# The last stage of a two-layer decoder: order of TensorE's products, statistics one step ahead, scores by chunks, and an output bias added by TensorE

## The reference

```
z      = layernorm(x)                      # only ahead of the first of the two
logits = compete_w . rms(z) + b            # 16 slots, per token
w      = softmax over tokens, of the 4 largest of each slot, else 0
ws     = rms(workspace + write(w . z))     # 16 x 512, the slots' content
att    = softmax(q(z) . k(ws)), 8 heads    # 128 tokens x 16 slots each
y      = z + out_proj(att . v(ws)) + out_b # out_b: the output bias
z'     = rms(y) * norm_post                # after the second: x + z' is stored
```

## Time and profile before

| | us |
|---|---|
| median of three timed runs | 4096.97 (4094.72 to 4097.59) |
| profiled execution | 4095.58 |
| its span | 4093.8 |
| last stage, TensorE busy in steps 1 to 15 | 803.30 of 936.90 |

### The profile page before, as it was taken

One profiled execution on the slowest core, in us unless ns is written; L12 is line 12 of the kernel. 1 busy time (PEld: TensorE's weight loads), 2 busy tenths in 40 slices (PEclk: granted clock), 3 DMA queues, 4 the chain that ended last, 5 costly groups with the idle time before them and its releaser, 6 DMA issues. The chain is left out here.

```text
span 4093.8 us, 86187 instructions
## 1 busy us (share of the span) xinstructions
PE 3644.9 (89%) x24323; PEld 1810.7 (44%) x24323; DVE 2875.2 (70%) x4470; ACT 2573.2 (63%) x6419; POOL 1785.7 (44%) x2216
## 2 busy tenths in 40 slices
PE   5999999999999994899999799999958878888886
PEld 1222222222222221778778444444436555465563
DVE  5888888888888883677777577777744454444545
ACT  2777777777777774677777577777734434344352
POOL 6444444444444430666665122222222543545535
PEclk9999999999999997899999999999979999999998
DMA  7777777777777762333332233333340120211102
GB/s 115 121 125 120 124 122 123 124 120 125 122 120 125 121 94 85 101 113 112 114 114 87 78 94 94 93 95 95 94 141 1 47 78 2 88 38 62 63 1 78
DMA packets 342548, 385.78 MB, mean 94 GB/s; under 512 B 58432, under 2 KB 223040, under 8 KB 342336
## 3 DMA queue, kind: packets, MB, share of 16 engines
q1 hardware_dynamic: 315712, 348.69, 39.4%
q10 hardware_dynamic: 26624, 34.63, 3.3%
HBM read 196.52 MB, written 84.93 MB: 69 GB/s over the span
## 5 line engine op out<-in xcount | busy, mean ns | idle before, releaser
L302 DVE TENSOR_REDUCE a_neg_max<-a_max_ps 128x2 f32<-128x1024 f32 x1024 | 1201.0, 1219 | 194.6 <-PE a_max_ps L354 169.8
L380 ACT ACTIVATE a_P<-a_ring_ps 128x512 f32<-128x512 f32 x2048 | 1084.6, 604 | 382.0 <-PE a_ring_ps L336 378.2
L354 PE MATMUL a_max_ps<-a_K,a_Q 96*128 96x512 bf16 x2048 | 621.1, 385 | 44.0 <-DMA a_K<-a_k_split 39.8
L336 PE MATMUL a_ring_ps<-a_Q,a_K 98*128 98x512 bf16 x2048 | 617.5, 382 | 5.7 <-DMA a_Q<-a_max_rows 3.5
L365 PE MATMUL a_pv_ps<-a_P,a_V 128*32 128x512 f32 x4096 | 544.9, 604 | 1.8 <-ACT a_out_sb L385 1.8
L336 PEld LDWEIGHTS a_ring_ps<-a_Q,a_K 98*128 98x128 bf16 x2048 | 158.9, 96 | 659.5 <-ACT a_P L380 585.5
L1163 ACT ACTIVATE c_P<-c_s_ps,c_bias 128x128 f32<-128x128 f32 x1024 | 361.5, 367 | 138.9 <-DVE c_bias L1035 130.2
L1092 PE MATMUL c_s_ps<-c_KD,c_qT 128*128 128x512 f32 x512 | 276.7, 622 | 33.5 <-ACT c_qT L1154 28.3
L1834 ACT ACTIVATE d_junk<-d_y 128x512 bf16<-128x512 f32 x128 | 80.6, 630 | 341.7 <-DVE d_y L1524 341.7
L256 POOL TENSOR_SCALAR a_var_eps<-a_mean_var 128x1 f32<-128x1 f32 x64 | 12.2, 190 | 648.1 <-DVE a_mean_var L318 647.9
L1031 DVE TENSOR_REDUCE c_neg_max<-c_s_ps 128x4 f32<-128x512 f32 x256 | 175.4, 685 | 163.7 <-PE c_s_ps L1093 163.7
(11 more groups left out here) (240 smaller groups left out, 7187.5 us busy)
## 6 DMA issues: line engine op xcount, KB each, us to landing
a_Q<-a_q_split SPq DMA_DIRECT2D x384, 128.0 KB
a_K<-a_k_split SPq DMA_DIRECT2D x384, 128.0 KB
heads_out<-a_out_sb ACTq DMA_DIRECT2D x128, 256.0 KB, 2.3
a_x_in<-in_x_dram SPq DMA_DIRECT2D x64, 256.0 KB, 3.6
a_c_in<-in_ctx_dram SPq DMA_DIRECT2D x64, 256.0 KB
a_cT_in<-in_ctxT_dram SPq DMA_DIRECT2D x64, 256.0 KB
b_x_in<-in_x_dram SPq DMA_DIRECT2D x64, 256.0 KB, 2.7
b_o_in<-heads_out SPq DMA_DIRECT2D x64, 256.0 KB
```

The costliest lines, as they stand in the source:

```text
L302: dve.tensor_reduce(neg_max[:, p, 2 * u:2 * u + 2], max_ps[u % 2][:, :, :], AX.X, ALU.max, negate=True).then_inc(max_taken, 1)
L336: pe.matmul(ring(s, use_of(k))[:, :], K[i][:, h, n:n + 128], Q[i][:, h, :], start=True, stop=True).then_inc(scores_filled, 1)
L354: last = pe.matmul(max_ps[u % 2][:, j, :], Q[i][0:KROW, h, m:m + 128], K[i][0:KROW, h, :], start=True, stop=True)
L380: act.activation(P[p][k // NT][:, k % NT, :], ring(s, use_of(k))[:, :], ACT.Exp, scale=SCALE).then_inc(exp_done, 1)
```

## The change

The bias add on GpSimd and its semaphore go; out_b is split at the start into three bf16 rows (at partitions 0, 32 and 64 of a 96-row tile that is otherwise 0), and each `mix` begins with a product of a 96 x 128 tile of ones with them, into the same bank, on which the f32 product accumulates. The layernorm statistics of a first f are made at the end of the step before; z is written in two halves, the first ahead of softmax(0). The scores go chunk by chunk (c outside, batch inside), and wait for six copies of A, for the last chunk for eight; the banks of the even and odd chunks change places (even now SC, odd F). On TensorE value_out(3) and mix(2) stand ahead of the wait for w_top, value_out(4) ahead of that for WT, mix(6) ahead of that for ws, mix(7) ahead of that for wsT; on VectorE final(6) and residual(7) stand ahead of kd, final(7) ahead of vd; ScalarE's copies and squares follow. Left out below: declarations, two memsets, and changed counts of `preset` and `const_ready`.

```diff
-body(Unit(0, k, 0), Unit(0, k, 1))
+body(Unit(0, k, 0), Unit(0, k, 1), Unit(0, k, -1))
...
-        + [(a_done, 2 * CK, i) for i in (0, 1, 4, 5)])
+        + [(a_done, 2 * CK, i) for i in (2, 3, 6, 7)])
...
-            add_bias(u, 0)
-            add_bias(u, 1)
         for b in range(NB):
-            if u.exists() and b >= 2:
-                add_bias(u, b)
             if u.exists() and b >= 1:
                 finish(u, b - 1)
...
-    def add_bias(u, b):
-
-        i, n = u.pair(), u.n()
-        if b == 0:
-            at_least(held, gT_done, n * 2 + 2)
-            at_least(held, xT_done, n * NB + NB)
-            if u.second():
-                held.wait_ge(x_sq_done, u.eight() * NB + NB)
-            held.wait_ge(g_done, n * 2 + 2)
-        pool.tensor_tensor(X[i][:, b, :], X[i][:, b, :], out_b_row[:, :], ALU.add).then_inc(x_biased, 1)
-        held.wait_ge(x_biased, n * NB + (b + 1))
...
+    dve.tensor_copy(out_b_part[:, :], out_b_row[0:96, :]).then_inc(const_ready, 1)
+    dve.wait_ge(const_ready, 4)
+    dve.tensor_copy(out_b_parts[0:1, :], out_b_part[0:1, :]).then_inc(const_ready, 1)
+    dve.tensor_tensor(out_b_row[0:96, :], out_b_row[0:96, :], out_b_part[:, :], ALU.subtract).then_inc(const_ready, 1)
+    dve.wait_ge(const_ready, 6)
+    dve.tensor_copy(out_b_part[:, :], out_b_row[0:96, :]).then_inc(const_ready, 1)
+    dve.wait_ge(const_ready, 7)
+    dve.tensor_copy(out_b_parts[32:33, :], out_b_part[32:33, :]).then_inc(const_ready, 1)
+    dve.tensor_tensor(out_b_row[0:96, :], out_b_row[0:96, :], out_b_part[:, :], ALU.subtract).then_inc(const_ready, 1)
+    dve.wait_ge(const_ready, 9)
+    dve.tensor_copy(out_b_parts[64:65, :], out_b_row[64:65, :]).then_inc(const_ready, 1)
...
+    def moments_of(f):
+
+        e = f.eight()
+        dve.wait_ge(x_loaded[f.pair()], f.turn() * 128 + 128)
+        at_least(dve, z_done, e * NB)
+        at_least(dve, x_ms_done, f.n())
+        for b in range(NB):
+            dve.bn_stats(stats[:, b, :], X[f.pair()][:, b, :]).then_inc(stats_done, 1)
+        for b in range(NB):
+            held.wait_ge(stats_done, e * NB + (b + 1))
+            dve.bn_aggr(moments[:, b, :], stats[:, b, :]).then_inc(moments_done, 1)
+    moments_of(Unit(0, 0, 0))
...
-            dve.wait_ge(x_biased, m + 1)
             dve.wait_ge(xb_filled, m + 1)
...
+        def normalise(batches):
+
+            dve.wait_ge(rstd_done, f.eight() + 1)
+            for b in batches:
+                dve.tensor_scalar(X[f.pair()][:, b, :], X[f.pair()][:, b, :], moments[:, b, 0:1], rstd[:, b:b + 1],
+                                  ALU.subtract, ALU.mult).then_inc(z_done, 1)
+
         first = f.exists() and not f.second()
         if first:
-
-            e = f.eight()
-            dve.wait_ge(x_loaded[f.pair()], f.turn() * 128 + 128)
-            at_least(dve, z_done, e * NB)
-            for b in range(NB):
-                dve.bn_stats(stats[:, b, :], X[f.pair()][:, b, :]).then_inc(stats_done, 1)
-            for b in range(NB):
-                held.wait_ge(stats_done, e * NB + (b + 1))
-                dve.bn_aggr(moments[:, b, :], stats[:, b, :]).then_inc(moments_done, 1)
+            normalise(range(0, NB // 2))
         if u.exists():
             softmax(0)
         if first:
-
-            dve.wait_ge(rstd_done, e + 1)
-            for b in range(NB):
-                dve.tensor_scalar(X[f.pair()][:, b, :], X[f.pair()][:, b, :], moments[:, b, 0:1], rstd[:, b:b + 1],
-                                  ALU.subtract, ALU.mult).then_inc(z_done, 1)
+            normalise(range(NB // 2, NB))
         if u.exists():
             softmax(1)
...
             residual(6)
+            final(6)
+            residual(7)
...
-            final(6)
-            residual(7)
+            final(7)
...
-        if u.exists():
-            final(7)
+        if after.exists() and not after.second():
+            moments_of(after)
...
-            pe.matmul(xb_ps[b % 2][:, :], attT[b // 4][:, b % 4, :], VO[b % 2][:, :], start=True, stop=True).then_inc(xb_filled, 1)
+            pe.matmul(xb_ps[b % 2][:, :], ones_rows[:, :], out_b_parts[:, :], start=True, stop=False)
+            pe.matmul(xb_ps[b % 2][:, :], attT[b // 4][:, b % 4, :], VO[b % 2][:, :], start=False, stop=True).then_inc(xb_filled, 1)
...
-                pe.wait_ge(a_done, n * 2 * CK + 2 * CK)
-                for b in range(half * 4, half * 4 + 4):
-                    for c in range(CK):
+                for c in range(CK):
+                    pe.wait_ge(a_done, n * 2 * CK + (8 if c == 3 else 6))
+                    for b in range(half * 4, half * 4 + 4):
                         last = pe.matmul(SC[half][:, b % 4 * 128:(b % 4 + 1) * 128], XT[i][:, c, b, :],
-                                         A[:, c, b].rearrange("p c s -> p (c s)"), start=(c == 0), stop=(c == CK - 1))
+                                         A[:, c, b].rearrange("p c s -> p (c s)"), start=(c == 0 and b % 4 == 0), stop=(c == CK - 1 and b % 4 == 3))
...
             mix(1)
+            value_out(3)
+            mix(2)
         if f.exists():
             ft = bank(pe, f, U_WT)
             pe.wait_ge(w_top_done, n * 2 + 2)
             pe.transpose(ft[:, 0:128], w_top[:, :], identf[:, :]).then_inc(wT_filled, 1)
         if u.exists():
-            value_out(3)
-            mix(2)
...
+            value_out(4)
...
-            value_out(4)
             mix(3)
...
             value_out(7)
+            mix(6)
...
-            mix(6)
+            mix(7)
         if f.exists():
             pe.wait_ge(wsT_done, n + 1)
             project(U_K, wk_sb)
-        if u.exists():
-            mix(7)
-        if f.exists():
             project(U_V, wv_sb)
...
-                pair = SC if c % 2 else [bank(pe, f, U_A + c + h) for h in range(2)]
-                if c == 3:
-                    pe.wait_ge(a_done, n * 2 * CK + 4)
+                pair = [bank(pe, f, U_A + c - 1 + h) for h in range(2)] if c % 2 else SC
+                if c == 2:
+                    pe.wait_ge(a_done, n * 2 * CK + 2)
...
+            values(3)
             squares(1)
-            values(3)
-            squares(2)
...
-            values(4)
+            squares(2)
+            values(5)
             squares(3)
-            values(5)
             squares(4)
...
             values(6)
+            values(7)
             squares(5)
-            values(7)
...
-                                   (SC[h] if c % 2 else F[(U_A + c + h) % 3])[:, :].rearrange("p (c b s) -> p c b s", c=CK, b=NB), ACT.Copy).then_inc(a_done, 1)
+                                   (F[(U_A + c - 1 + h) % 3] if c % 2 else SC[h])[:, :].rearrange("p (c b s) -> p c b s", c=CK, b=NB), ACT.Copy).then_inc(a_done, 1)
```

More of the change, by code:

```diff
@@ L1249, in workspace_ffn @@
         ws_first = sb("ws_first", [128, C])
+        out_b_parts, ones_rows = sb("out_b_parts", [96, C], BF16), sb("ones_rows", [96, 128], BF16)
+        out_b_part = sb("out_b_part", [96, C], BF16)
         neg_half = sb("neg_half", [128, NB])
@@ L1353, in _, with step @@
                 sp.sem_inc(out_stored[i], 16)
-            def step(f, u):
+            def step(f, u, after):
                 if u.exists() and u.second():
@@ L1378, in _ @@
             n = 0
-            for dst, value in ((neg_half[:, :], -0.5), (cw[:, :, :], 0.0), (lg[:, 128:136], -FAR), (chosen[:, :], -FAR), (WT[:, :, :], 0.0),
+            for dst, value in ((neg_half[:, :], -0.5), (cw[:, :, :], 0.0), (lg[:, 128:136], -FAR), (chosen[:, :], -FAR), (WT[:, :, :], 0.0), (out_b_parts[:, :], 0.0), (ones_rows[:, :], 1.0),
                                (vd[0][:, :, :, :, :], 0.0), (vd[1][:, :, :, :, :], 0.0)):
@@ L1482, in _ @@
             dve.wait_ge(small_in, 16 * (7 + 2 * NB))
-            dve.wait_ge(preset, 7)
+            dve.wait_ge(preset, 9)
             dve.tensor_tensor(cw[:, :, 0:S], cw_in[:, :, :], pre_col[:, :].unsqueeze(2).to_broadcast([128, CK, S]), ALU.mult).then_inc(const_ready, 1)
@@ L1657, in _, with step @@
         def _(pe):
-            pe.wait_ge(const_ready, 3)
-            def step(f, u):
+            pe.wait_ge(const_ready, 10)
+            def step(f, u, after):
                 def value_out(b):
@@ L1879, in step @@
                 if u.exists():
+                    values(3)
                     squares(1)
-                    values(3)
-                    squares(2)
+                    values(4)
                 if f.exists():
```

8 lines of the change are left out of this document (4 added, 4 removed).

## The result

Median 4041.59 us (four runs, 4037.83 to 4044.45) against 4097.28 for the kernel before on the same chip: a ratio of 0.9864 (95% interval 0.9848 to 0.9879), 55.7 us less, where 70 were forecast. The profiled execution took 4037.83 around a span of 4036.0, 57.8 shorter than the earlier trace rows.

The account below looks back on a forecast made before the run. Bound: a ring through VectorE, ScalarE and GpSimd, 3.6 us a turn, with TensorE's holes worth filling only down to it. 58.4 + 14.7 - 2.8 - 0.3 = 70 less, giving a 4027 us median; range 3978 to 4062.

Parts of the forecast that it names:

- (e): Second-u steps, first mix to first bias product: ring turns in 3.6, B = M + 32.2; 38.1 us off six steps.
- S to M: First score product to first product into xb_ps: six f-first steps lose 2.8 us, M = S + 22.4.
- B to S: First bias product (L1802) to next scores: chunked scores overlap the last copy of A, 14.7 us off.
- M to B: First product into xb_ps to the first bias product (L1802): 58.4 us off in all.
- (d): Rest of the step from L1775 on: hole before L1785 gone, B = M + 32.0; six first-u steps 8.3 us less.
- (a): Last operation of the top-4 weights, without GpSimd's bias add beside it: 0.285 us instead of 0.96, 0.65 off.
- (b): The bf16 bias product added to each mix: 0.25 us, eight per step, four of them on the path.
- the rival at 1.12: Each bias product costs like the f32 pair it precedes, 1.12 us, so the kernel is slower: 4112; chance 0.05.
- (c): Ring of residual, square, mean, final at 3.6 us a turn holds the gT copies; TensorE idles 1.2 before L1775.
- the rival of TensorE as the only bound: Ring and x landing hide behind TensorE's 52.5 us a step: 3954; chance 0.15, half-way versions included.
- Collision: In second-u loop steps final and GpSimd's store add collide, the turn is 4.4, B = M + 34.9: 4052; chance 0.13.
- The loop edges: At the two loop edges TensorE waits 3 us for its own next instructions; no gain taken there.

Follow-up runs that it names:

- e3: Changed kernel with VectorE's two gT copies moved from behind residual(3) to between residual(2) and final(2): 4022.5 us.
- e1: Changed kernel with four output buffers instead of two: 4022.7 us.
- f1: Changed kernel with GpSimd's store add moved ahead of the next batch's mean and power, still two output buffers: 4012.0 us.
- a2: Changed kernel with the scores part undone (all of A first, batch by batch, old banks): 4051.1 us.
- d1: Kernel before with only the bias by TensorE and the scores by chunk: 4032.8 us.
- e2: Changed kernel with softmax(0) put back ahead of all eight z in f-first steps: 4029.6 us.
- a3: Changed kernel with the orders of products, squares, values and kd put back as before: 4039.1 us.
- b1: Kernel before with only the bias part: TensorE adds the output bias, GpSimd's bias adds gone: 4037.1 us.
- g1: Changed kernel with store add ahead of the mean, softmax(0) ahead of all z, early gT copies, x reload behind residual: 3969.5 us.

## Why the prediction was right, and where it was not

Direction and range held, the size was 14 too large: three terms fell short, by 13.1 (e), 14.1 (S to M) and 2.0 (B to S), and others made up for part of it. Of those, 11 us in M to B are (d); 2.9 are a shift of the start of step 1 that the change may not have made, which is luck.

- *(a) w_top.* Right: 0.286 in every step (forecast 0.285).
- *(b) Bias product.* Right: 0.23 (3526.50 to 3526.73, forecast 0.25), and the rival at 1.12 is out.

```profile
L1597 DVE TENSOR_SCALAR d_w_top<-d_w_raw,d_w_inv x16: 285/286/288, 3066.3 to 3945.2; 128x128 f32<-128x128 f32 x16
```

```profile
3526.50 0.39 PE L1681 MATMUL d_xb_ps<-d_out_b_parts,d_ones_rows 96*128 96x512 bf16 x1
3526.73 1.02 PE L1682 MATMUL d_xb_ps<-d_VO,d_attT 128*128 128x512 f32 x2
```

- *(c) The ring and the gT hole.* Right in kind: the time taken from the early hole returns before L1781, 1.5 with a first u (forecast 1.2) but 2.9 with a second, where the half clock follows it. That "gT waits for residual 3, a ring of 3.6 that the diff leaves" was right against the rival of TensorE as the only bound.
- *(d) First u and outside.* B came at M + 31.0 and M + 30.0, not 32.0: 11 us better. mix 6 ended at M + 22.4 instead of 22.85, and the four transposes, mix 7 and two projections took 8.6 instead of 9.1; in steps 1 and 14 the ring turns in 3.3, which the earlier trace rows did not show, being from the loop. By the forecast's own sign, M to B under 31 means that the ring isn't binding. At 30.98 that is just met: TensorE is busy 29.5 of it, and its one wait, 1.5 for gT, was worth only 0.5 a step in e3.
- *(e) Second u.* This step failed: "With the eight bias adds gone the ring turns in 3.6 here too". It took GpSimd for the only holder. The second was in the kernel's text, two output buffers and an add that follows the next batch's mean; at the old turn of 4.7 the store was back in time but for final(7) (5 waits, 1.3 us together). Now every other turn from residual 2 on takes 4.9 to 6.2, B is M + 34.4 in the mean instead of 32.2, 38.1 became 25.0, and e1 gives back 14.0, all of it, the clock's share included.
- *Collision.* The rival named the right sign and place (1.59 and 1.83 in step 8) and its B = M + 34.9 is near the 34.4 measured; its reason, a GpSimd that is idle earlier, was not the one: `final` comes late, held by the store, and e1 and f1 both remove the collision in the loop by taking the transfer's wait away.
- *B to S.* 12.7 of 14.7. That S coming sooner leaves the landing where it is, and so costs S to M, was in the forecast's S to M (it set the landing against the new S); the runs give its size, 12.5 of 19.6 in a2 and 7.6 of 14.1 in d1.
- *S to M.* 16.9 lost, 2.8 forecast. The landing-to-M figure was right (21.2 forecast; 24.75 - 3.33 = 21.4 in the mean), the landing was not: S + 0.8 to 1.6 forecast, 3.3 measured, since it hangs on residual 7 of (e): M + 32.9 in the mean, 28.9 forecast. That the z order costs was seen, but "a gain of 6" without it doesn't follow from the forecast's own figures: 21.2 against 19.2 behind the landing is 2.0 in each of six steps, 12, and a gain of 9. Measured: 12, 9.6 of it in S to M (e2).
- *Which part pays.* The forecast gave the filled holes a share that they don't keep: the spread takes 9.2 off M to B and loses 7.3 in S to M (a3). The bias alone gives as much as the whole change (b1).
- *A slip.* L1775's end at 18.2 and the four products of 1.0 and 1.25 make 22.7, not 22.85.
- *The loop edges.* "TensorE waits for its own next instructions" is not shown: the profile marks these 3 us only as "issue", a wait for nothing that it shows.

## What to carry to other kernels

Before moving work into a hole, ask what the hole's releaser was waiting for: here nearly half of the two holes was another engine's adds. When a ring gets faster, look up every buffer and transfer that its new turn overtakes; a store that was back in time at 4.7 us a turn is not at 3.6, and what it holds by half a microsecond can then collide and lose another. And moving one line in an off-path engine's queue (the store add ahead of the mean) gave more than reordering the products of three engines.

## What the runs showed of the hardware

**Which VectorE operation suffers beside GpSimd.** `final`, with its operands in SBUF, loses the rest of GpSimd's add when it starts with or after it: in the changed kernel 32 of its 64 runs on a store buffer do, take 0.89 to 1.86 us, and each ends 0.55 us after the add. Started 0.04 ahead of the add it still loses (1.86); 0.25 or 0.34 ahead (e1) it keeps 0.75, and the add takes 1.64 and 1.54 instead of 1.27. residual, which reads one operand from PSUM, keeps 0.69 beside an add at 1.27 (f1, and no residual in that run took longer, 44 of them beside an add). The Trainium skill, "SBUF — State Buffer", section "Who interferes with whom", says that a VectorE instruction with at most one SBUF input, outside the two-port modes, does not contend with GpSimd; the traces agree, and f1's gain depends on it.

**The store's round trip.** In 8 of the 13 waits of `final` on a store the 256 KB were back 2.1 us after the issue, in the others after 2.3 to 3.6 (steps 3 to 12 of the changed kernel). The Trainium skill, "DMA: Bandwidth & Descriptors", section "Anatomy of one DMA — SWDGE (gpsimd) path", fits transfers that GpSimd issues with about 2 us fixed and the bytes at 436 GB/s; an estimate by it is 2.6 us. These stores are issued by SyncE, for which the fit isn't made; what was measured lies on both sides of it.

**TensorE's clock behind a pause.** At the loop edges TensorE is idle for about 3 us, and the profile shows nothing that it waits for. In step 10 behind such an edge the granted clock was 0.92 and S to M 19.16; in step 2, with no edge, 1.00 and 17.76. Stretch, length, busy times and counts, clock:

```profile
3148.80:3166.56 17.76, 16.52 (x154) 12.88 (x155) 6.51 (x11) 13.71 (x32) 3.97 (x4) 1.00 0.01 2
...
3631.14:3650.30 19.16, 17.93 (x154) 14.28 (x154) 6.55 (x11) 12.89 (x30) 3.97 (x4) 0.92 0.01 3
```

It doesn't follow each time: in b1 the same edge ahead of step 6 left 1.00 and 17.76. That part of the stretch ran at 1.2 GHz instead of 2.4 costs 1.4 us here, and 2.9 in g1 (step 6, S to M 20.70 at 0.85). The hole of 2.9 us before the write product is the other place: 1.4 to 1.7 us in five of six steps of the changed kernel, none where the hole is 1.5 (e1) or gone (e3).
